# Patch weights prepared first and image 0 embedded meanwhile; single-pass scatter; new instruction orders

## The reference, cut to what matters

```
p = img2patches(x, 16, 16)                     # 196 x 768
h = layernorm(layernorm(p, ln1) @ W + b, ln2)  # patch embedding, 768 -> 192
a = layernorm(h)
h = h + causal_attention_with_relative_keys(a) # 12 heads of 16
f = layernorm(h)
# routed block on f:
normed = ln(f, g1, b1); scores = sigmoid(normed @ Wr + br)
idx    = 29 tokens with the lowest scores      # 0.15 * 196
attn   = full attention over normed            # kept only in the rows idx
mix    = (normed + scores * pooled) @ Wm + bm  # kept in all other rows
h'     = f + where(row in idx, attn @ Wo + bo, mix)
h      = h + (h' + gelu(ln(h', g2, b2) @ W1 + bf1) @ W2 + bf2)
```

## Time and profile before

| what | value |
|---|---|
| time, median of 3 runs | 5560.41 us (5558.65 to 5562.08) |
| time of the profiled execution | 5558.0 us |
| span of the profiled execution | 5556.2 us |
| instructions | 146436 |
| PE busy | 5185.8 us, 93% of the span |
| DVE busy | 4301.6 us, 77% |
| ACT busy | 3799.2 us, 68% |
| POOL busy | 2762.3 us, 50% |
| 16 DMA engines | 32 GB/s on average, about a quarter busy |

### The profile page before, as it was taken

One profiled execution on the slowest core, in us unless ns is written; L12 is line 12 of the kernel. 1 busy time (PEld: TensorE's weight loads), 2 busy tenths in 40 slices (PEclk: granted clock), 3 DMA queues, 4 the chain that ended last, 5 costly groups with the idle time before them and its releaser, 6 DMA issues.

```text
span 5556.2 us, 146436 instructions
## 1 busy us (share of the span) xinstructions
PE 5185.8 (93%) x48224; PEld 4863.6 (88%) x48224; DVE 4301.6 (77%) x12888; ACT 3799.2 (68%) x12542; POOL 2762.3 (50%) x3415
## 2 busy tenths in 40 slices
PE   3899999999999999999999999999999999999998
PEld 3888889889888888888988888888898888888887
DVE  2787777777778777777777777877777777787776
ACT  1667767776776776777677677677767767767775
POOL 4454554555455455455445545545544554554552
PEclk8999999999999999999999999999999999999999
DMA  3222222222222222222222222222222222222220
GB/s 52 37 29 30 35 31 30 32 34 30 29 37 29 30 36 30 30 32 34 30 29 37 29 30 36 30 30 33 34 30 29 37 30 29 36 30 30 33 33 6
DMA packets 229237, 175.82 MB, mean 32 GB/s; under 512 B 28423, under 2 KB 228699, under 8 KB 229207
## 3 DMA queue, kind: packets, MB, share of 16 engines
q1 hardware_dynamic: 218913, 172.63, 23.5%
q10 hardware_dynamic: 9110, 1.84, 0.2%
q0 software_dynamic: 1184, 0.97, 0.1%
HBM read 156.11 MB, written 19.27 MB: 32 GB/s over the span
## 4 chain that ended last, share of the span: by engine, by line
PE 59%; ACT 14%; DVE 13%; issue 6%; DVEq 5%; ACTq 2%; POOL 1%; POOLq 0%
PE banks L636 8%; PE banks L646 8%; PE banks L695 7%; PE banks L628 6%; PE banks L684 5%; PE banks L924 5%; DVEq L1359 4%; PE banks L620 3%; ACT p L1540 3%; PE banks L820 3%; DVE a_row L1127 3%; ACT L1518 3%; PE banks L719 2%; ACT gstore L1525 2%; DVE qk_parts L1341 2%
## 5 line engine op out<-in xcount | busy, mean ns | idle before, releaser
L1540 ACT ACTIVATE p<-banks,negmax 98x98 f32<-98x98 f32 (+1 forms) x3072 | 1141.8, 381 | 208.8 <-DVE negmax L1172 166.6
L517 POOL TENSOR_TENSOR p<-p,rden 98x392 f32<-98x392 f32 (+1 forms) x768 | 895.9, 1188 | 778.4 <-DVE rden L1186 778.4
L695 PE MATMUL banks<-tokw,x_sb 128*98 128x193 f32 x4096 | 765.8, 340 | 16.0 <-DVEq L1114 16.0
L695 PEld LDWEIGHTS banks<-tokw,x_sb 128*98 128x98 f32 x4096 | 716.0, 254 | 16.9 <-DVEq L1114 16.1
L1172 DVE TENSOR_REDUCE negmax<-banks 98x2 f32<-98x392 f32 (+1 forms) x1152 | 625.7, 553 | 131.0 <-PE banks L684 126.7
L526 POOL TENSOR_TENSOR gstore<-gstore 96x784 f32<-96x784 f32 x128 | 236.4, 1847 | 894.5 <-ACT gstore L1525 894.5
L684 PE MATMUL banks<-kz,qk_parts 128*98 128x392 f32 x2304 | 647.4, 385 | 0.0
L1540 ACT ACTIVATION_READ_ACCUMULATOR p<-banks,negmax 98x1 f32 x3072 | 619.4, 202 | 0.0
L924 PE MATMUL banks<-w,gparts 128*98 128x192 f32 x4608 | 508.8, 260 | 0.0
L719 PE MATMUL banks<-ident,p 98*98 98x98 f32 x4608 | 495.8, 251 | 3.8 <-ACTq L1544 2.9
L636 PE MATMUL banks<-z3Ts,w_split 128*128 128x196 f32 x3840 | 490.3, 280 | 1.4 <-DVE z3Ts L1143 1.4
(11 more groups left out here) (293 smaller groups left out, 12777.9 us busy)
## 6 DMA issues: line engine op xcount, KB each, us to landing
x_sb<-in_x SPq DMA_DIRECT2D x384, 196.0 KB, 4.8
x_sb<-in_x SPq DMA_DIRECT2D x384, 189.0 KB, 7.7
out<-out_row SPq DMA_DIRECT2D x128, 147.0 KB
pT<-in_L_tok_W SPq DMA_DIRECT2D x6, 96.0 KB
pT<-in_L_ffn_W ACTq DMA_DIRECT2D x1, 576.0 KB
gstore<-in_L_ffn_W SPq DMA_DIRECT2D x1, 384.0 KB
gstore<-in_L_ffn_W ACTq DMA_DIRECT2D x2, 192.0 KB
p<-in_L_attn_w_attn ACTq DMA_DIRECT2D x2, 96.0 KB
```

Of the source, the lines that this page charges most:

```text
L517: last = gp.tensor_tensor(heads, heads, rden[:, g, t].unsqueeze(2).broadcast_to([HT, 4, w]), ALU.mult)
L695: last = mm(bank[b][0:HT, t * (D + 1):(t + 1) * (D + 1)], xf[:, a:a + (HT - 1) * PS + 1:PS], tokw[:, q], start=t == 0 and q == 0, stop=q = ...
L1540: sc.activation((p1 if t else p0)[0:HT, 4 * g + s], bank[b][0:HT, w * i:w * i + w], ACT.Exp, bias=negmax[:, g, t, s:s + 1], accum_out=den[ ...
```

## The change

- **Start.** The 18 loads of the patch weights go first, on SP and ACT. All other loads are dealt to SP and ACT; POOL issues none. PE and DVE start on the patch weights as soon as these and the constants are there; POOL clears kz, v_sb, ctxT, nsel, qb1, ao and selT after the constants (`stores_zeroed`). PE and DVE finish the patch weights (`tok_ready`) before the others, and PE calls step(-3) at its end of `tok_ready`, not of `w_ready`. ACT calls step(-3) at `w_ready`, no longer at `p1_zeroed`; DVE clears p1, pT0 and pT1.
- **Scatter.** `selT` and `ao` become float32r. DVE writes `ao` as a rounded part and a rest (a copy, a drain and a subtraction for one addition), PE multiplies both parts. The bias `bo - bm` becomes a row of `fwo` that meets a row of ones in `ctxT`, so that `fbo` goes.
- **Orders.** The pieces of a step stand in new orders on PE, DVE and ACT. On POOL `h1_with_bias` moves from the start of the step to the place after the second reciprocal root of image l.

```diff
-        by_sp, by_act, by_gp = loads[0::3], loads[1::3], loads[2::3]
+        tok_by_sp, tok_by_act = loads[0:n_tok:2], loads[1:n_tok:2]
+        by_sp, by_act = loads[n_tok::2], loads[n_tok + 1::2]
...
+            pe.wait_ge(one["tok_ready"], 1)
...
                     for t in range(2):
-                        last = mm(bank[5][0:HT, t * D:(t + 1) * D],
-                                  selT[:, HT * t:HT * t + HT], ao[:], start=True,
-                                  stop=True)
+                        for part in range(2):
+                            last = mm(bank[5][0:HT, t * D:(t + 1) * D],
+                                      selT[:, HT * t:HT * t + HT], ao[:, part],
+                                      start=part == 0, stop=part == 1)
...
-                    ve.tensor_tensor(ao[0:SELP], bank[4][0:SELP, 0:D], fbo[:],
-                                     ALU.add).then_inc(sem["ao_sb"], 1)
+                    ve.tensor_copy(ao[0:SELP, 0], bank[4][0:SELP, 0:D])
+                    ve.drain()
+                    ve.tensor_tensor(ao[0:SELP, 1], bank[4][0:SELP, 0:D],
+                                     ao[0:SELP, 0].bitcast(F32),
+                                     ALU.subtract).then_inc(sem["ao_sb"], 1)
...
+            step(-3, -2, -1, 0, True, False, False, False, False)
+            pe.wait_ge(one["w_ready"], 1)
             steps(pe, step)
...
             ve.drain().then_inc(one["w_ready"], 1)
+            ve.memset(p1[:], 0.0)
+            ve.memset(pT0[KX:128], 0.0)
+            ve.memset(pT1[KX:128], 0.0)
+            ve.drain().then_inc(one["p1_zeroed"], 1)
```

More of the change, by code:

```diff
@@ L541, in step @@
                     rstd(mv_y[:, :, 1], ve2[:], rstd2[:], "y_rstd")
+                if front:
+                    h1_with_bias()
                 if front:
@@ L935, in step @@
                 if front:
-                    keys()
+                    queries()
                 if back:
@@ L939, in step @@
                 if front:
-                    queries()
+                    keys()
                 if back:
@@ L944, in step @@
                     values()
+                if head:
+                    embed(0,0,QH)
+                if tail:
+                    mlp_cols()
                 if back:
@@ L995, in step @@
                 if front:
+                    causal("A3")
                     causal("B1")
+                if back:
+                    attn_out()
+                if front:
+                    causal("A4")
+                    causal("A5")
                 if tail:
@@ L1062, in _ @@
                                  split[name][:, 0::2].bitcast(F32), ALU.subtract)
+            ve.wait_ge(one["tok_sums"], 1)
+            for q in range(QH):
+                ve.scalar_tensor_tensor(tokw[0:KX, q, 0:D], bank[0][0:KX, 0:D], -1.0 / PD,
+                                        tokw[0:KX, q, 0:D], ALU.mult, ALU.add)
+            ve.tensor_tensor(tok_bias[:], bank[1][0:HT, 0:D], tok_brow[:], ALU.add)
+            ve.drain().then_inc(one["tok_ready"], 1)
             ve.wait_ge(one["w_sums"], 1)
@@ L1389, in step @@
                     routing_scores()
-                if front:
-                    query_parts()
-                if back:
                     rank_tokens()
@@ L1432, in step @@
                     maxima(8)
+                    inverse_sums(2)
+                if back:
+                    context2()
+                if front:
+                    transposed("A0")
+                    transposed("A2")
+                if back:
+                    context2_cols()
                 if head:
@@ L1435, in step @@
                 if front:
-                    inverse_sums(2)
-                    transposed("A0")
-                if back:
-                    context2()
-                    context2_cols()
-                if front:
-                    transposed("A2")
                     transposed("A3")
@@ L1449, in step @@
                 if tail:
-                    gelu_parts(2)
+                    gelu_parts(1)
+                if back:
+                    attn_out()
                 if front:
@@ L1454, in step @@
                     attention_input()
-                if back:
-                    attn_out()
+                if tail:
+                    gelu_parts(2)
                 if front:
@@ L1473, in _ @@
         def _(sc):
+            for dst, src in tok_by_act:
+                sc.dma_start(dst, src).then_inc(one["tok_in_act"], 16)
             sc.wait_ge(one["zeroed"], 1)
@@ L1621, in step @@
                 if front:
-                    queries()
                     keys()
-                if back:
-                    values2()
-                    keys2()
-                if front:
-                    load_table(ACT.Exp)
-                if back:
-                    exp_scores()
+                    values()
                 if head:
@@ L1633, in step @@
                 if front:
-                    values()
+                    load_table(ACT.Exp)
+                    queries()
                 if back:
-                    gathered()
+                    keys2()
                 if tail:
                     mlp_cols_hi()
+                if back:
+                    values2()
+                    exp_scores()
                 if front:
@@ L1641, in step @@
                     softmax(1)
+                if back:
+                    gathered()
+                if front:
                     softmax(2)
+                    softmax(3)
                 if back:
@@ L1678, in step @@
                     block_input()
+            sc.wait_ge(one["w_ready"], 1)
+            step(-3, -2, -1, 0, True, False, False, False, False)
+            sc.wait_ge(one["p1_zeroed"], 1)
+            sc.wait_ge(one["stores_zeroed"], 1)
             steps(sc, step)
```

165 lines of the change are left out of this document (82 added, 83 removed).

## The result

The changed kernel takes 5585.66 us (median of 6 runs, 5582.9 to 5587.85). The kernel before took 5561.2 us beside it (6 runs, 5558.65 to 5562.38). The ratio is 1.0044, 95% interval 1.0031 to 1.0057: 0.44% slower, where the forecast was 0.5% faster. The time lies inside the range of 5450 to 5630 us. Every piece of the forecast step came, in its place and within 0.42 us; their sum came out on the other side of the old step. None of the three signs of being wrong appeared (the gap before S0, what holds `h1_stats`, the clock). The step and the first squares (84.18 us, near 81 forecast) lie outside what was written down for them.

A forecast was written before the change was run, and what follows sets the result against it. PE's order with its waits was taken to bound the 42.09 us step. From 5558.0 us, loop -18, start -12 and first front steps +3 gave 5531, as a median 5533 us, 0.5% faster; range 5450 to 5630.

The forecast's parts named there:

- three signs of being wrong: S0's gap under 0.8 or over 2 us; h1_stats not held up by POOL; clock leaving 1.00 inside the loop.
- What bounds the kernel: Loop step: PE's order with its waits is the 42.09 us step; a new order can win at most 2.83 us.
- Item 2: Before S0: five ACT pieces, then DVE's query_parts; S0 starts at 12.11 us, a new PE gap of 1.34 us.
- Items 3 to 6: S0 to embed(1) 9.88 us; wait to up0 3.19; up0 to context2's end 4.28; late image to projection 8.32.
- Item 7: Step's end: PE takes 3.97 us from projection; DVE's tail ends 12.35 to 12.68 us after context2, giving 41.8 to 42.1.
- The scatter: Single-pass products win PE 0.30 us a step; DVE pays a copy and drain, about 0.35 us; half eaten by its tail.
- h1_with_bias: On POOL before normalised(2): hidden in a wait for DVE; without that cover it would add 1 us to the chain.
- The start: Before the loop: w_ready moves from 87.95 to 80.9 us, loads 4 us later; wins 12 us, between 5 and 16.
- A: Rival: PE's gaps shrink; with none left a step is 38.96 us, some 5160 us; chance of below 5500: 0.12.
- D: Rival: the gap before S0 lowers PE's clock in each step, +200 us, 5730 us; chance 0.07.
- B: Rival: DVE's tail at its upper end and slower fill eat the scatter's and start's gains; 5550 to 5571 us; chance 0.16.
- C: Rival: DVE and POOL collide more often; with 0.7 us lost a step is 42.65 us, 5620 us; chance 0.20.

The follow-up runs named there:

- e4: Changed kernel with ACT's queries moved right after its values, ahead of squares and the Exp table: 5481.10 us, ratio 0.9859.
- e7: Changed kernel with DVE's embedding split, the operations that read bank 6 ahead of maxima7 and their statistics after it: 5529.79 us, ratio 0.9948.
- e6: Changed kernel with DVE's embedding_normalised moved from after context2_cols to before context2: 5571.79 us, ratio 1.0023.
- e3: Changed kernel with the float32 scatter put back (one copy of ao), keeping new start and orders: 5583.81 us, ratio 1.0044.
- e12: The e10 kernel with the float32 scatter put back, without DVE's second copy of ao: 5435.08 us, ratio 0.9769.
- e11: The e10 kernel with ACT's queries ahead of its values and the rounded part of ao written by ACT: 5436.56 us, ratio 0.9774.
- e9: Changed kernel with the edits of e4 and e7, PE's A1 right behind A0, and the rounded ao written by ACT: 5479.78 us, ratio 0.9855.
- e10: Changed kernel with the edits of e4 and e7 together: 5429.90 us, ratio 0.9764.
- e1: Changed kernel with the old orders on all four engines, keeping the new start and scatter: 5547.31 us, ratio 0.9977.

## Why the prediction was wrong

**What bounds the kernel** was right: the step of PE with its waits is the time, every 0.01 us of it 1.25 us. e4 and e7 took out 0.82 and 0.41 us of bracket, and the step fell by 0.82 and 0.43.

**Item 2 failed, by its size.** Its mechanism was right: five ACT pieces, then DVE, then S0, 12.11 us; it measured 12.53. Of the 0.42, 0.24 is the ACT row, 6.87 for 6.63. I had taken 0.1 off each recorded length for the overlap of neighbours. Here the pieces stand nearly end to end (2021.27 + 2.60 = 2023.87, the next at 2023.89; 2024.59 + 1.51 = 2026.10, the next at 2026.12), and only v and the dummy overlap. Another 0.17 is the time until ACT starts: the item says that DVE's late tail costs 0.23 at `score`, beside ACT's row and so for nothing. PE does take 4.60 us from the queries to `score` (2016.53 to 2021.13), not 4.37. But `routed_cols` stands between queries and keys in the new order and waits for z0 first, by 0.09 us, and with some 0.08 of slower starts around it 0.17 of the 0.23 lies ahead of the last of the keys, and so ahead of all of ACT's row. e6 shows the term by itself: with DVE's tail earlier, the keys come as summed, and S0 at 12.35.

**Items 3 to 6** measured 9.83, 3.30, 4.33 and 8.37 against 9.88, 3.19, 4.28 and 8.32. Items 3 to 5, which enter the step, are 0.11 over together; item 6 lies inside item 7.

**Item 7** was 12.35 to 12.68 after the end of `context2`, 12.49 in the step that was taken, and measured 12.38: 0.42 + 0.11 - 0.11 is the whole miss of 0.42 us a step. My step of 41.8 to 42.1 was this item's range laid upon items 2 to 5 as if these had none. That is the second fault: six legs, each worked out to some 0.1 us, gave a range of 0.3 us around a gain of 0.14 us. Item 2's errors alone, 0.42 x 125 = 52 us, are three times the loop's forecast gain of 18 us. The chance of slower should have been near that of faster.

**The scatter** measured 0.29 us a step on PE (0.30 taken), and DVE's copy cost it again, in the new orders in full (e3) or but for 0.04 us (e12). I had booked PE's 0.30 inside item 7, where DVE's bounds decide, so nothing of it was in the forecast's 41.95; the text that says it is "half eaten" was too kind.

**h1_with_bias** at its new place showed no cost: no wait for it appears in the step.

**The start** won 9.6 of 12 us. The loads ended at 51.27, 5.0 us later where 4 were taken; from there to w_ready, DVE's last row before 84.18, it was 32.8 us (30.6 taken). These 2.2 us are the larger of the start's two errors. By the rule cited there from the Trainium skill ("DMA: Bandwidth & Descriptors", Issuing engines are not separate DMA queues) the loads would have ended no later, and the trace shows 5.0 us later. The list of the loads was reordered in the same edit as POOL was taken from it, the two were not run apart, and which of them costs the 5.0 us stays open.

**The rivals.** A, PE's own work decides: no; PE is 3.41 us a step above 38.96. D, the clock falls: no, 1.00 in the loop. B, the order gives nothing, names the right place (small excesses on items 2 to 7) with too small a sum. C, collisions of DVE and POOL: 5620 us did not come, and one of the two collisions went (a_row 0.67 instead of 1.36), so the further loss that C named did not come. Its mechanism is real: the rows put what e6 and e11 did not win, and what e9 lost, down to such meetings, though no run takes one out by itself. The rule cited for it from the Trainium skill ("SBUF — State Buffer", Who interferes with whom), by which the two lock each other out for a whole instruction, agrees in kind: DVE's subtraction takes 1.22 to 1.29 us instead of 0.57, a_row 1.09 to 1.37 instead of 0.67. In length it does not quite: in the changed kernel a_row starts 0.26 us before the record of h2b ends and still takes 0.67 us. POOL's records are rough, so this may be the record and not the rule.

**Cause.** Shown by e4, e7 and e10: the new orders lose through the gaps before S0 and before `up0`; with the first one cut by 0.82 us the same kernel is 1.4% faster than before, with both cut 2.4%. The forecast had both gaps, and nearly at their size (1.34 and 0.96 us; the brackets show 1.30 and 0.91). What turned its small gain into a loss is the 0.42 us of item 2.

## What to carry to other kernels

In a hand-made order, look for the piece that feeds the bound engine and stands behind work that nobody waits for: moving ACT's copy of the queries past 2.9 us of squares and table load, one line, was worth 105 us, where the start and the scatter together had won 13 (e1). When a step is summed from six legs, add an error for each leg before comparing with a gain of a third of a per cent, and do not subtract an overlap from a record unless the same two neighbours show it. And before work is taken from DVE or moved on it, look at what POOL does at the new moment: the next operation may arrive in the middle of one of POOL's and end no earlier than before.

## What the runs showed of the hardware that I had not expected

An additional instruction can pay for itself by its timing: DVE's second copy of ao (0.41 us) let a_row start 0.75 us after POOL's h2b instead of 0.33, and it took 0.67 instead of 1.10 us (e10 against e11): it ended 1.42 or 1.43 us after h2b's start in both. The collisions also lengthen POOL: L552 took 1.54 us beside DVE's L1390 (e9) and 1.00 alone. And the first embedding ran at half the clock (columns as in the earlier trace rows), although PE had been busy since 53.93 us; most of that were 52 products of one column each:

```profile
69.81:75.30 5.49, 5.46 (x17) 4.43 (x16) 5.18 (x24) 0.00 (x0) 0.00 (x0) 0.50 0.00 1
```

The clock was granted at 0.50, 1.2 GHz, and the 16 products of `embed` took 5.46 us; in the loop they take 2.95. In the kernel before, where PE had stood idle for 16.04 us ahead of them, they took 4.60.
